# Causal attention in a language-model tower on one core: scores as three one-pass products with a masked minimum, two orders exchanged, and inverse roots by one GpSimd power

## The reference, cut to what matters

```python
h = h + _L1_attn_ref(_layernorm(h, axis=-1), L1_attn_Wq, L1_attn_Wk, L1_attn_Wv, L1_attn_Wo, L1_attn_bo)
h = h + _L1_ffn_ref(_layernorm(h, axis=-1), ...)

def _L1_attn_ref(x, Wq, Wk, Wv, Wo, bo):
    b, t, e = x.shape                       # 64, 256, 128
    h = Wq.shape[1] // e                    # 8 heads of 128
    q, k, v = ((x @ W).reshape(b, t, h, e).transpose(0, 2, 1, 3) for W in (Wq, Wk, Wv))
    dot = jnp.einsum('bhqe,bhke->bhqk', q / math.sqrt(e), k)
    dot = jnp.where(jnp.tril(jnp.ones((t, t), dtype=bool))[None, None], dot, -jnp.inf)
    out = jnp.einsum('bhqk,bhke->bhqe', jax.nn.softmax(dot, axis=-1), v)
    return out.transpose(0, 2, 1, 3).reshape(b, t, h * e) @ Wo + bo
```

## Time and profile before

| | |
|---|---|
| median of 3 runs | 2606.75 us (2601.83 to 2608.33) |
| the profiled execution | 2612.21 us, of which 2610.5 us are the span from its first to its last instruction |
| busy share of the span | PE 88%, PEld 77%, DVE 72%, ACT 65%, POOL 54% |
| granted TensorE clock, mean | 0.96 of full speed |

### The profile page before, as it was taken

The page is one execution under the profiler, slowest core; times in us unless marked ns, Lnnn a source line. Parts: engine busy times, 40 slices in busy tenths (PEclk is TensorE's granted clock), DMA queues, the critical chain, the costliest instruction groups (busy, mean ns, idle before and its releaser), DMA issues.

```text
span 2610.5 us, 59252 instructions
## 1 busy us (share of the span) xinstructions
PE 2309.8 (88%) x16748; PEld 2017.1 (77%) x16764; DVE 1869.5 (72%) x8460; ACT 1692.1 (65%) x5249; POOL 1419.6 (54%) x1724
## 2 busy tenths in 40 slices
PE   4999977667777599999999999999999999999966
PEld 3877865444444499999999999899898999999855
DVE  4787767555445278888888887777778888788733
ACT  2777744122112287777787777888787888778744
POOL 6544100556556368778887774344443677447443
PEclk8999989888888799999999999999999999999988
DMA  2566686333333431111111126555554888468577
GB/s 74 195 234 209 222 213 97 101 109 122 112 118 117 131 94 50 46 46 43 48 51 46 46 75 170 156 161 163 156 154 110 242 231 243 133 194 243 147 218 226
DMA packets 357908, 361.96 MB, mean 139 GB/s; under 512 B 35603, under 2 KB 301692, under 8 KB 357584
## 3 DMA queue, kind: packets, MB, share of 16 engines
q1 hardware_dynamic: 321376, 272.95, 37.9%
q0 software_dynamic: 33472, 78.98, 9.2%
q10 hardware_dynamic: 2736, 6.25, 0.7%
...
## 4 chain that ended last, share of the span: by engine, by line
PE 64%; DVE 15%; issue 7%; another core or an unknown queue 4%; POOL 3%; ACT 3%; DMA 2%; ACTq 0%; SPq 0%; DVEq 0%; POOLq 0%
PE bank L2210 7%; PE bank L2289 6%; PE bank L2303 6%; PE bank L2221 5%; PE bank L2209 4%; PE bank L2236 4%; PE bank L2256 4%; PE bank L2238 4%; PE bank L2237 4%; PE bank L2264 3%; PE bank L2178 3%; PE bank L2084 2%; POOL rows L910 2%; PE bank L2162 2%
## 5 line engine op out<-in xcount | busy, mean ns | idle before, releaser
L948 POOL DMA_INDIRECT zbuf<-pc,kb x248 | 251.7, 1015 | 242.6 <-DVE pc L1863 189.7
L942 POOL DMA_INDIRECT spread_rows<-kb,pos x248 | 253.7, 1023 | 199.6 <-DVE pc L1863 105.1
L2210 PE MATMUL bank<-xT,gT 128*128 128x256 f32 x1024 | 306.1, 381 | 0.0
L1666 DVE COPY pr_place<-bank 128x384 f32<-128x384 f32 x512 | 281.6, 550 | 19.6 <-PE bank L2221 13.8
L1645 DVE TENSOR_REDUCE nmax<-bank 128x1 f32<-128x128 f32 x512 | 144.1, 282 | 195.8 <-PE bank L2210 108.9
L1153 ACT ACTIVATE pr_place<-bank,nmax 128x128 f32<-128x128 f32 x512 | 188.8, 369 | 136.4 <-DVE nmax L1646 122.6
L2303 PE MATMUL bank<-wvo_part,x_part 128*128 128x512 f32 x768 | 267.8, 457 | 1.1 <-ACT vo_place L1241 1.0
L1163 ACT ACTIVATE bank<-causal 128x384 f32<-128x384 f32 x512 | 253.4, 495 | 19.4 <-PE bank L2394 3.3
L2221 PE MATMUL bank<-ident,pr_place 128*128 128x128 f32 x1536 | 251.8, 273 | 9.9 <-DVE pr_place L1666 9.1
L2221 PEld LDWEIGHTS bank<-ident,pr_place 128*128 128x128 f32 x1536 | 196.9, 140 | 77.1 <-DVE pr_place L1659 14.5
L2289 PE MATMUL bank<-x_part,wqk_part 128*128 128x256 f32 x1536 | 245.8, 296 | 1.2 <-DVE x_part L1806 1.2
...
## 6 DMA issues: line engine op xcount, KB each, us to landing
...
```

Source lines behind the costliest of these rows:

```text
L942: pool.indirect_dma_start(out=spread_rows, out_offset=bass.IndirectOffsetOnAxis(ap=pos[:, k, j:j + 1], axis=0), in_=xr4s[g % 2][:, k, j], ...
L948: pool.indirect_dma_start(out=zbuf, out_offset=bass.IndirectOffsetOnAxis(ap=xu_at(t)[:, C + 1:XW].bitcast(U32), axis=0), in_=yu[:, t % YR] ...
L1666: dve.tensor_copy(prT[:, h % 2], t_bank(u)[:, 0:3 * P]).then_inc(prT_ready, 1)
L2210: pe.matmul(s2[:, P:3 * P], g[:, P:2 * P], xT3[:, p], start=False, stop=True, skip_group_check=True)\
```

## The change

1. The fold exchanges its two operands, so that g belongs to the key side. ACT copies g of two heads as its high part, DVE makes the rest (`low`, a subtraction of 512 columns), and the scores of two heads are six fp32r matmuls: three of 256 columns for the first query tile (bank 4) and three of 512 for the second (bank 3). The stationary operand is now x, whose two parts exist already; `xT3` and its copy go.
2. ACT no longer writes masks. `maxima` is one instruction for each query tile that adds `causal` to the scores, negates them, writes them to SBUF and gives their minimum (`tensor_tensor_reduce`), and `exps` reads SBUF with scale -1.
3. The copy of the transposed probabilities moves from DVE (`turn`) to ACT (`probs_copied`).
4. The Newton steps of the two layer norms are replaced by one addition on DVE and one power with exponent -0.5 on POOL (`prepared_root`, `gates_root`). Those of the part before slot 0 of this pipeline stay.
5. All four lags grow by one; scores are made in even slots only, and PE does `turns` and `sums` at the start of a slot, the products at the end of odd ones. `finish` comes before the normalisation in its slot, `split` at the start of its slot.

```diff
-        h3 = sb("h3", [P, 2, 2, C])
+        h3 = wqk[:].rearrange("p h c -> p (h c)")[:, 0:4 * C].rearrange("p (q j c) -> p q j c", q=2, j=2)
...
-        gT = sb("gT", [P, 2, 4 * P])
+        g_part = [sb(f"g_part{k}", [P, 2, 4 * P], F32R) for k in range(2)]
...
-        S_LAG, N_LAG, T_LAG, O_LAG = 1, 2, 4, 5
+        S_LAG, N_LAG, T_LAG, O_LAG = 2, 3, 5, 6
...
+            def prepared_root(n):
+                pool.wait_ge(prep_step, 4 * (n + 1))
+                pool.tensor_tensor(r3[:, 0], r3[:, 1], mhalf[:, 0:2], ALU.pow).then_inc(roots_made, 1)
+
+            def gates_root(g):
+                pool.wait_ge(d_step, GATE_STEPS * g + TG + 2)
+                pool.tensor_tensor(r4[:, 0], r4[:, 1], mhalf[:], ALU.pow).then_inc(roots_made, 1)
...
-                act.activation(xT3[:, p], bank[VBANK][:, 0:2 * P], ACT.Copy)
...
                 act.wait_ge(max_ready, u + 1)
-                if u >= PRN:
...
-                s2 = bank[SBANK[h % 2]]
-                act.activation(pr[:, u % PRN, 0:P], s2[:, 0:P], ACT.Exp, bias=nmax[:, h % 4, 0:1],
+                act.activation(pr[:, u % PRN, 0:P], pr[:, u % PRN, 0:P], ACT.Exp, bias=nmax[:, h % 4, 0:1], scale=-1.0,
                                accum_out=rsum[:, h % 4, 0:1])
-                act.activation(pr[:, u % PRN, P:3 * P], s2[:, P:3 * P], ACT.Exp, bias=nmax[:, h % 4, 1:2],
...
-                if u + 2 < NB * H1:
-                    set_mask(u + 2)
-
-            def set_mask(u):
+
+            def probs_copied(u, h):
+                act.wait_ge(prT_mm, u + 1)
                 if u >= 2:
-                    act.wait_ge(exp_ready, u - 1)
-                act.activation(bank[SBANK[u % 2]][:, 0:3 * P], causal[:], ACT.Copy).then_inc(mask_set, 1)
+                    act.wait_ge(head_mm, u - 1)
+                act.activation(prT[:, h % 2], t_bank(u)[:, 0:3 * P], ACT.Copy).then_inc(prT_ready, 1)
 
...
+                            act.activation(g_part[0][:, h // 2 % 2], bank[GBANK][:, :], ACT.Copy).then_inc(g_ready, 1)
+                        if there(u - T_LAG):
+                            probs_copied(u - T_LAG, (h - T_LAG) % H1)
...
+                n_.done(dve.tensor_scalar(r3[:, 1], mv3[:, :, 1], EPS, None, ALU.add))
...
-                prep_now["steps"].wait()
+                dve.wait_ge(roots_made, prep_root_at(n))
...
-                dve.wait_ge(s_mm, u + 1)
-                s2 = bank[SBANK[h % 2]]
-                dve.tensor_reduce(nmax[:, h % 4, 0:1], s2[:, 0:P], AX.X, ALU.max, negate=True)
-                dve.tensor_reduce(nmax[:, h % 4, 1:2], s2[:, P:3 * P], AX.X, ALU.max, negate=True).then_inc(max_ready, 1)
+                dve.wait_ge(s_mm, u // 2 + 1)
+                if u >= PRN:
+                    dve.wait_ge(prT_mm, u - PRN + 1)
+                early = bank[SBANK[1]][:, (h % 2) * P:(h % 2 + 1) * P]
+                late = bank[SBANK[0]][:, (h % 2) * 2 * P:(h % 2 + 1) * 2 * P]
+                dve.tensor_tensor_reduce(out=pr[:, u % PRN, 0:P], in0=early, in1=causal[:, 0:P], scale=-1.0, scalar=3e38,
+                                         op0=ALU.add, op1=ALU.min, accum_out=nmax[:, h % 4, 0:1])
+                dve.tensor_tensor_reduce(out=pr[:, u % PRN, P:3 * P], in0=late, in1=causal[:, P:3 * P], scale=-1.0,
+                                         scalar=3e38, op0=ALU.add, op1=ALU.min, accum_out=nmax[:, h % 4, 1:2])\
+                    .then_inc(max_ready, 1)
 
             def inverses(u, h):
...
+            def low(m):
+                dve.wait_ge(g_ready, m + 1)
+                dve.tensor_tensor(g_part[1][:, m % 2], bank[GBANK][:, :], g_part[0][:, m % 2].bitcast(F32), ALU.subtract)\
+                    .then_inc(low_ready, 1)
...
+                        if h == 6 and n + 1 < NB:
+                            split(n + 1, 1 - p)
...
                         if there(u - N_LAG):
                             inverses(u - N_LAG, (h - N_LAG) % H1)
                         if there(u - S_LAG):
                             maxima(u - S_LAG, (h - S_LAG) % H1)
-                        root_step()
+                        if h == O_LAG - 1 and there(u - O_LAG):
+                            finish(n - 1, 1 - p, i, p)
+                        if h % 2 == 0 and n < NB:
+                            low(4 * n + h // 2)
...
-                        if there(u - T_LAG):
-                            turn(u - T_LAG, (h - T_LAG) % H1)
...
-                    pe.matmul(bank[3][:, 0:C], wT[:, 0], wT[:, 1], start=True, stop=True)
+                    pe.matmul(bank[3][:, 0:C], wT[:, 1], wT[:, 0], start=True, stop=True)
...
-            def scores(u, h, p, n):
-                s2 = bank[SBANK[h % 2]]
-                g = gT[:, h // 2 % 2, (h % 2) * 2 * P:(h % 2 + 1) * 2 * P]
-                pe.wait_ge(g_ready, 4 * n + h // 2 + 1)
-                pe.wait_ge(mask_set, u + 1)
-                pe.matmul(s2[:, 0:P], g[:, 0:P], xT3[:, p, 0:P], start=False, stop=True, skip_group_check=True)
-                pe.matmul(s2[:, P:3 * P], g[:, P:2 * P], xT3[:, p], start=False, stop=True, skip_group_check=True)\
-                    .then_inc(s_mm, 1)
+            def products(n, h, p):
+                for k in range(2):
+                    for m, (a, b) in enumerate(PARTS):
+                        ins = pe.matmul(bank[GBANK][:, k * 2 * P:(k + 1) * 2 * P], wqk_part[a][:, h + k], x_part[b][:, p],
+                                        start=(m == 0), stop=(m == 2))
+                ins.then_inc(g_mm, 1)
+
+            def scores(m, p):
+                pe.wait_ge(low_ready, m + 1)
+                if m >= 1:
+                    pe.wait_ge(max_ready, 2 * m)
+                for k, (a, b) in enumerate(PARTS):
+                    pe.matmul(bank[SBANK[1]][:, 0:2 * P], x_part[b][:, p, 0:P],
+                              g_part[a][:, m % 2].rearrange("c (k t) -> c k t", k=2)[:, :, 0:P], start=(k == 0), stop=(k == 2))
+                for k, (a, b) in enumerate(PARTS):
+                    ins = pe.matmul(bank[SBANK[0]][:, :], x_part[b][:, p, P:2 * P], g_part[a][:, m % 2], start=(k == 0), stop=(k == 2))
+                ins.then_inc(s_mm, 1)
...
+                        if there(u - T_LAG):
+                            turns(u - T_LAG, (h - T_LAG) % H1)
+                        if there(u - O_LAG):
+                            sums(u - O_LAG, (h - O_LAG) % H1, p if h >= O_LAG else 1 - p, n if h >= O_LAG else n - 1)
...
-                        if there(u - S_LAG):
-                            scores(u - S_LAG, (h - S_LAG) % H1, p if h >= S_LAG else 1 - p, n if h >= S_LAG else n - 1)
+                        if h % 2 == 0 and there(u - S_LAG):
+                            scores((u - S_LAG) // 2, p if h >= S_LAG else 1 - p)
...
-                        if there(u - T_LAG):
-                            turns(u - T_LAG, (h - T_LAG) % H1)
-                        if there(u - O_LAG):
-                            sums(u - O_LAG, (h - O_LAG) % H1, p if h >= O_LAG else 1 - p, n if h >= O_LAG else n - 1)
+                        if h == 7 and n + 1 < NB:
+                            pe.wait_ge(parts_split, n + 4)
+                            pe.wait_ge(low_ready, 4 * n + 4)
+                            products(n + 1, 0, 1 - p)
+                        elif h % 2 and h < 7 and n < NB:
+                            if (p, h) == (1, 1) and gated(i - 1):
+                                pe.wait_ge(xT4_ready, i)
+                            if (p, h) == (1, 3) and gated(i - 1):
+                                pe.wait_ge(lg4_ready, i)
+                            pe.wait_ge(low_ready, 4 * n + h // 2 + 1)
+                            products(n, h + 1, p)
```

92 lines of the change are left out of this document (29 added, 63 removed).

## The result

The kernel after takes 2651.74 us (median of 4 runs, 2648.26 to 2657.61), the kernel before 2607.54 on the same chip: a ratio of 1.0163 with a 95% interval of 1.0135 to 1.0191. The change makes it slower by some 44 us, where 2598 was forecast. The profiled execution spans 2651.0 us, 40.5 more than that of before.

The account below looks back on a forecast made before the run. PE was taken to set the time, with DVE close behind. First half +16, second half -23 and roots -2 gave -9 us: 2603 profiled, a median of 2598; range 2562 to 2655, the forecast's own 2585 to 2620.

Parts of the forecast that it names:

- What PE saves: PE, attention: scores of a pair 1.06 us against 1.32, 2.08 saved a round, and a 0.61 wait for DVE's copy gone.
- M: DVE's time for the two combined maxima instructions of a head: taken as 0.74 us, between 0.53 and 1.20.
- my own slope: Each 0.1 us more for a head's maxima costs 11 us in the first half and 3 in the second, 14 us.
- my sign: The forecast would be wrong if a head's maxima on DVE cost outside 0.65 to 0.90 us.
- my chances: Forecast 0.40, PE keeping its gain 0.33, loop setting first half 0.24, slow power 0.03; faster 0.45, same 0.17, slower 0.38.
- The loop of the score banks: First half: a pair's scores wait until DVE read the last pair; waits at bias matmul and sums, 3.68 us a round.
- `low`: DVE gains a 512-column subtraction, 0.60 us in each even slot.
- The roots: Newton steps off DVE: -2 us at the start; power on POOL 0.3 us, bounds 0.195 to 0.615, three a round hidden.
- the last rival: POOL's power, if over 3 us, delays first-half normalisations; at 5 us each +96, 2695 us; chance 0.03.
- The first half: Attention's first 16 rounds: waits of 3.68 against savings of 2.08 and 0.61, +1.0 us a round, +16 us.
- The second half: Attention's last 16 rounds: PE's unit steps cover most waits; 2.08 saved less 0.64, 1.44 a round, -23 us.
- What would show it: PE's first-half share about 91%, its rounds about 1 us longer, second-half rounds 1.4 shorter, bias matmul waiting; wrong at 97%.

Follow-up runs that it names:

- late_products: Kernel after with most scatters in odd slots, slot 6's bias and sums behind its scores, products behind even slots' sums, ahead of scores: ratio 1.0100 to before.
- scores_mid: Kernel after with most scatters in odd slots and scores ahead of the sums in all even slots: 2442.62 us, 0.9821 of before.
- low_small2: Kernel after with `low` working on 8 of its 512 columns after the first two products: ratio 0.9932 to before.
- newton: Kernel after with the twelve Newton steps back on DVE in place of both POOL powers: ratio 1.0053 to before.
- before_power: Kernel before with one part of the change alone, both inverse roots by the POOL power: ratio 0.9934 to before.
- second chip: Kernel after, unchanged, run on another chip than the first measurement: ratio 1.0024 to before on that chip.
- the third: Kernel after, unchanged, run once more on a third chip: ratio 1.0023 to before on that chip.

## Why the prediction was wrong, step by step

- *What PE saves.* Right. Without its waits a round is 39.96 before (40.83 less the 0.87 of slot 7, which I had at 0.61) and 38.0 in after (42.4 less 4.4), 1.9 to 2.0 less where 2.08 was forecast; the rest lies in waits under 0.1. A pair costs its 1.06 us also behind an fp32 sum. The rows seem to give 1.14, but there the first matmul starts 0.03 behind the last of the sum in place of 0.11, and the second 0.20 behind the first in place of 0.12: the sum of both distances is the same.
- *M.* Mis-sized: 0.56, not 0.74, at the lower end. By my own slope that should have given about 2573, and by my sign (M outside 0.65 to 0.90) the forecast was wrong. M was the hinge of my chances, and yet the kernel got slower: the waits didn't come from it.
- *The loop of the score banks.* The step that failed in the first half. I worked out two ends of it, the bias matmul and the sums, and got waits of 3.68 us a round. Measured are 4.4, but 0.9 of them at the bias (p = 1, where I had 1.91, and none at p = 0) and none at the sums. The rest stand where I put none: 2.3 at the turns for GpSimd and 0.9 at the products for `low`. I had cut the path at the exponentials and taken normalisation and turn as covered by the higher lags. But all lags grew alike: scores and turn are three slots apart in both kernels (lags 1 and 4, then 2 and 5), and inside the slot the turn moved to the start and the scores behind turn and sums. late_products shows what the place of the scores is worth to the turns, scores_mid what it is worth to the products. That 3.68 lay near 4.4 is luck.
- *`low`.* Costed as load on DVE, not as the thing that frees the one bank of the products. In low_small2 it is worth 1.4 us a round.
- *The roots.* Power outside my bounds: 0.72 and 1.04 us against 0.195 to 0.615. Two of my signs for the last rival came, a power above a microsecond and DVE waiting for it (L1710 in after, 0.35 us once a round). "Hidden" was near enough in the new order all the same (newton gains 0.2 us a round without it), but the steps that it removes weren't seen as what they are in before_power, 16 us. I had counted 2.
- *The first half.* +16 forecast, +24.5 measured.
- *The second half.* The other step that failed, on the chip of the record: the term of -23 came out as +11.9. PE's completions come late there, and no step of mine had this, though the rows of the kernel before show DVE released 17 times by something unknown, 58.1 us. In the profiled executions the miss is 49.5 us, and 34.9 of them are this term. On the second chip it is -22.1 (the third has the same rounds), but for another reason than mine: I had 2.08 saved less a wait of 0.64 at the bias matmul. That matmul doesn't wait there. By the start distances the 2.08 are saved whole, and some 0.5 of small waits stand elsewhere, the largest (some 0.25) at products behind `vo`. The agreement of the number is luck.
- *What would show it.* PE's share fell to 94%, between my 91% and the 97% that I called wrong; rounds of the first half grew by 1.6, not 1.0. The bias matmul hardly waited in p = 0: by the text's own test the picture of the loop was wrong.
